# Causal softmax with 8-wide heads: mask and maximum from matrix products and reductions to fused vector operations

## What is computed

```python
q = _rope(q)
k = _rope(k)
att = jnp.einsum('bhqd,bhkd->bhqk', q, k) * (1.0 / np.sqrt(D))
causal = jnp.tril(jnp.ones((T, T), dtype=bool))
att = jnp.where(causal, att, -jnp.inf)
att = jax.nn.softmax(att, axis=-1)
y = jnp.einsum('bhqk,bhkd->bhqd', att, v)
```

## Time and profile before

| | |
|---|---|
| median of 3 runs | 2307.49 us (2306.52 to 2309.47) |
| the profiled execution | 2311.73 us, its span 2309.9 us |
| busy over the whole span | TensorE 2175.3 us (94%), VectorE 1691.0 (73%), ScalarE 1782.4 (77%), GpSimd 1432.2 (62%) |
| the stage of the change | about 213 to 546 us |

### The profile page before, as it was taken

One profiled execution on the slowest core, in us unless ns is written; L12 is line 12 of the kernel. 1 busy time (PEld: TensorE's weight loads), 2 busy tenths in 40 slices (PEclk: granted clock), 3 DMA queues, 4 the chain that ended last, 5 costly groups with the idle time before them and its releaser, 6 DMA issues. The chain is left out here.

```text
span 2309.9 us, 67166 instructions
## 1 busy us (share of the span) xinstructions
PE 2175.3 (94%) x22598; PEld 1606.6 (70%) x22598; DVE 1691.0 (73%) x3594; ACT 1782.4 (77%) x6112; POOL 1432.2 (62%) x1432
## 2 busy tenths in 40 slices
PE   6987999999698999999999999899999999999999
PEld 4984666665696788864788864675788864788863
DVE  5554888886554889973899974575899963899964
ACT  4774888986575999982899982556999982999982
POOL 4663777773663788860788860572788850888850
PEclk8997999999799999999999999999999999999999
DMA  6111000000113000000000000000000000000000
GB/s 248 43 40 42 2 0 0 0 1 24 40 43 120 9 9 7 9 0 5 9 9 7 9 1 0 2 0 6 9 9 7 9 0 5 9 9 7 9 1 37
DMA packets 22566, 45.93 MB, mean 20 GB/s; under 512 B 5344, under 2 KB 13792, under 8 KB 22048
## 3 DMA queue, kind: packets, MB, share of 16 engines
q1 hardware_dynamic: 17440, 34.01, 4.4%
q0 software_dynamic: 4992, 10.23, 1.5%
HBM read 24.44 MB, written 11.40 MB: 16 GB/s over the span
## 5 line engine op out<-in xcount | busy, mean ns | idle before, releaser
L279 POOL TENSOR_TENSOR space<-space 128x512 f32<-128x512 f32 x256 | 325.7, 1272 | 268.5 <-DVE space L382 268.1
L274 POOL TENSOR_TENSOR space<-space 128x512 f32<-128x512 f32 x256 | 267.6, 1045 | 126.1 <-ACT space L315 125.9
L329 ACT ACTIVATE space<-psum,space 128x128 f32<-128x128 f32 x1024 | 337.0, 385 | 1.7 <-DVE space L373 1.7
L1011 POOL TENSOR_TENSOR space<-space 128x256 f32<-128x256 f32 (+1 forms) x256 | 221.4, 886 | 85.2 <-DVE space L1113 83.1
L176 PE MATMUL psum<-big,space 128*128 128x256 f32 x1024 | 266.1, 382 | 6.8 <-issue 3.4
L268 POOL TENSOR_TENSOR space<-space 128x512 f32<-128x512 f32 x256 | 266.9, 1042 | 7.9 <-DVE space L353 7.3
L373 DVE TENSOR_REDUCE space<-psum 128x4 f32<-128x512 f32 x256 | 177.1, 692 | 98.0 <-PE psum L191 93.7
L1057 ACT ACTIVATE space<-psum,space 128x128 f32<-128x128 f32 (+1 forms) x512 | 210.3, 442 | 1.8 <-DVE space L1106 1.7
L329 ACT ACTIVATION_READ_ACCUMULATOR space<-psum,space 128x1 f32 x1024 | 201.8, 197 | 0.0
L176 PEld LDWEIGHTS psum<-big,space 128*128 128x128 f32 x1024 | 174.6, 190 | 28.4 <-issue 15.2
L676 ACT ACTIVATE big<-psum,wt 128x512 f32<-128x512 f32 (+1 forms) x96 | 65.4, 686 | 152.0 <-PE psum L653 151.9
(11 more groups left out here) (196 smaller groups left out, 5483.3 us busy)
## 6 DMA issues: line engine op xcount, KB each, us to landing
big<-early SPq DMA_DIRECT2D x1, 6944.0 KB, 27.5
rows<-space SPq DMA_DIRECT2D x16, 256.0 KB, 2.4
z<-token_y SPq DMA_DIRECT2D x16, 256.0 KB, 5.3
space<-z SPq DMA_DIRECT2D x64, 64.0 KB, 1.9
space<-z SPq DMA_DIRECT2D x64, 63.8 KB, 2.1
big<-late SPq DMA_DIRECT2D x1, 3114.0 KB, 13.7
x<-x_t SPq DMA_DIRECT2D x4, 512.0 KB, 5.2
x_final<-x SPq DMA_DIRECT2D x8, 256.0 KB, 2.1
```

What stands on the lines that cost most here:

```text
L274: pool.tensor_tensor(x, x, rn[:, (j - 1) % 2, :].unsqueeze(2).to_broadcast([P, 8, LD]), ALU.mult).then_inc(scaled, 1)
L279: pool.tensor_tensor(t3[:, j % 2, :], t1[:, j % 2, :], t2[:, j % 2, :], ALU.add).then_inc(summed, 1)
L329: ins = act.activation(pr[:, j % 2, h, t * P:(t + 1) * P], s_ps[h][:, t * P:(t + 1) * P], ACT.Exp, bias=nm[:, j % 2, h, t:t + 1], accum_ou ...
L1011: ins = pool.tensor_tensor(x, x, rl[:, ee % 2, t, :].unsqueeze(2).to_broadcast([P, 2, c1 - c0]), ALU.mult)
```

## The change

The mask leaves TensorE. The table `tri_q` becomes 384 columns wide (the triangle, zeros, the triangle) and holds -1e25 for masked places. In place of two reductions VectorE issues four fused operations `tensor_tensor_reduce`, one for each tile and head. Each adds the table (from SBUF) to the scores (from PSUM), multiplies by -1, writes the result to `pr` in SBUF, and gives the minimum of what it wrote, which is the negated maximum, to `nm`. ScalarE then takes the exponential in place in `pr`, with scale -1. The banks of scores are free once VectorE has read them (`nm_ready`), no more after the exponentials (`p_ready`). The wait for a free slot of `pr` (`pt_ready, s - 3`) moves from ScalarE to VectorE.

```diff
+FAR = 1e25
...
-    b["tri_q"] = (1 - seen.T) * MASKED
+    b["tri_q"] = np.concatenate([1 - seen.T, np.zeros((P, P)), 1 - seen.T], 1) * -FAR
...
                     if at_least(s, 2):
-                        pe.wait_ge(p_ready, s - 1)
-                    for n in range(2):
-                        mm(bank[n].rearrange("p (a n) -> p a n", a=4)[:, 0:4:2, :], g.ident[:, :], g.tri_q.unsqueeze(1).to_broadcast([P, 2, P]),
-                           start=True, stop=False, skip_group_check=True)
+                        pe.wait_ge(nm_ready, s - 1)
                     for t, cols in ((0, slice(0, P)), (1, slice(P, TRI))):
                         for n in range(2):
                             q = 2 * (e % 2) + n
                             r = slice(32 * q, 32 * q + 32)
-                            ins = mm(bank[n][:, cols], qz[r, k, jj, t * P:(t + 1) * P], qk[r, k, T:T + (t + 1) * P], start=False, stop=(t == 1), skip_group_check=True)
+                            ins = mm(bank[n][:, cols], qz[r, k, jj, t * P:(t + 1) * P], qk[r, k, T:T + (t + 1) * P], start=(t == 0), stop=(t == 1), skip_group_check=True)
...
                     act.wait_ge(nm_ready, u + 1)
-                    if at_least(u, 4):
-                        act.wait_ge(pt_ready, u - 3)
                     for t, (c0, c1) in enumerate(((0, P), (P, TRI))):
                         for h in range(2):
-                            ins = act.activation(pr[:, ee % SLOTS, h, c0:c1], s_ps[ee % 2][h][:, c0:c1], ACT.Exp,
-                                                 bias=nm[:, ee % 2, t, h:h + 1], accum_out=ls[:, ee % 2, t, h:h + 1])
+                            x = pr[:, ee % SLOTS, h, c0:c1]
+                            ins = act.activation(x, x, ACT.Exp, scale=-1.0, bias=nm[:, ee % 2, t, h:h + 1], accum_out=ls[:, ee % 2, t, h:h + 1])
...
+                    if not isinstance(s, int):
+                        for n in (-1, 1, 3):
+                            dve.compute_val(s - n)
+                    dve.wait_ge(v_zero, 1)
                     dve.wait_ge(s_ready, s + 1)
                     if at_least(s, 2):
                         dve.wait_ge(p_ready, s - 1)
-                    dve.tensor_reduce(nm[:, e % 2, 0, :], s_pair[e % 2][:, :, 0:P], AX.X, ALU.max, negate=True)
-                    dve.tensor_reduce(nm[:, e % 2, 1, :], s_pair[e % 2][:, :, P:TRI], AX.X, ALU.max, negate=True).then_inc(nm_ready, 1)
+                    if at_least(s, 4):
+                        dve.wait_ge(pt_ready, s - 3)
+                    for t, (c0, c1) in enumerate(((0, P), (P, TRI))):
+                        for h in range(2):
+                            ins = dve.tensor_tensor_reduce(pr[:, e % SLOTS, h, c0:c1], s_ps[e % 2][h][:, c0:c1], g.tri_q[:, c0:c1], -1.0, FAR,
+                                                           ALU.add, ALU.min, nm[:, e % 2, t, h:h + 1])
+                    ins.then_inc(nm_ready, 1)
```

More of the change, by code:

```diff
@@ L871, in small_head_softmax @@
     s_ps = ((g.bank[2], g.bank[3]), (g.bank[4], g.bank[5]))
-    s_pair = (g.bank_pair2, g.bank_pair4)
     pt_ps = (g.bank[6], g.bank[7])
@@ L1142, in free @@
     def free(eng, bank):
-        last = ((turned, B), (out_ready, B), (p_ready, U), (p_ready, U), (p_ready, U), (p_ready, U), (pt_low, U), (pt_high, U))
+        last = ((turned, B), (out_ready, B), (nm_ready, U), (nm_ready, U), (nm_ready, U), (nm_ready, U), (pt_low, U), (pt_high, U))
         eng.wait_ge(*last[bank])
```

## The result

The changed kernel takes 2298.06 us (median of 9 runs, 2294.92 to 2305.4) against 2307.97 us for the one before (9 runs on the same chip): ratio 0.9964, 95% interval 0.9953 to 0.9975. It is faster by 9.9 us. Forecast were 2311 us and no gain, with a chance of 0.33 for faster, so the sign is missed, although 2298 lies inside the range.

A forecast was written before the change was run, and what follows sets the result against it. TensorE was taken to bound the softmax stage, with VectorE taking its place after the change. Even part +8, last batch -2, first rounds -4 and end rounds +1 gave +3 us on the median 2307.5: 2311 us, range 2286 to 2359.

The forecast's parts named there:

- even part: 14 softmax batches from 242 to 522 us: VectorE's 20.4 + 0.2 us a batch against TensorE's 20.04, +8 us.
- last batch, and the ends: Last batch, without projection or rotation, still paced by TensorE: -2 us; last round's fused operations with nothing beside them: +0.53.
- first rounds, and the first fused operation: Seven low-clock rounds each lose mask products of 0.56 us, -4 us; first round's fused operations with nothing beside them, +0.53.
- The bound before: Softmax stage before the change: TensorE sets the pace, busy 20.00 of 20 us, a batch taking 20.04 us.
- What TensorE gives up: Two mask products a round leave TensorE, 2.5 us a batch, so it needs 17.5 and waits 2.5 to 3.
- The exchange on VectorE: Fused operations 1.10 us plus reads 0.36 replace reductions of 0.93: +0.53 us a round, VectorE 16.2 to 20.4 a batch.
- 0.2 us a batch for the waits between engines: Allowance in the even batches for VectorE waiting on ScalarE's exponentials, tight in the round with no extra operation.
- The price of SBUF: ScalarE's exponentials reading SBUF cost +0.024 us each, 0.8 us a batch, giving 18.6 of 20.4 us busy, hidden.
- Rival 1: VectorE's accumulator read is nearly free: 2292 us with 0.05 a read, 2283 with 0.03; chance 0.22.
- Rival 2: Each fused operation and read on VectorE holds the next for its full length: 2.10 us a round, 2384 us; chance 0.10.
- Rival 3: VectorE's fused operation has a fixed part 0.05 to 0.10 us larger than a reduction: 2335 to 2359 us; chance 0.17.
- Rival 4: TensorE stays longer at the low clock: ten such rounds more +16 us, a whole stage +200; chance 0.04.

The follow-up runs named there:

- before_total_first: Kernel before the change, with GpSimd's sum of the rotation (L997) moved ahead of its product in that round: 20.04 us a batch, 1.0001 of before.
- no_mask: Kernel before the change, with its two mask products on TensorE left out and nothing in their place: 18.68 us a batch, 0.9900 of before.
- exp_from_psum: Changed kernel with exponentials taken from the unmasked scores in PSUM, fused operations kept, banks held until the exponentials are done: 19.69 us a batch, 0.9977 of before.
- both_masks: Changed kernel with TensorE's two mask products kept ahead of the scores: 20.28 us a batch, 1.0013 of the kernel before.
- split_dve: Changed kernel with VectorE's copy of the transposed probabilities cut in three: 19.95 us a batch, 0.9982 of the kernel before.
- psum_in_place: Changed kernel with fused operations writing back into the PSUM bank of scores and exponentials reading PSUM again: 20.47 us a batch, 1.0022 of the kernel before.
- less_dve: Changed kernel with VectorE's copy of the transposed probabilities cut to 128 of 384 columns: 18.83 us a batch, 0.9908 of the kernel before.
- after_again: The changed kernel itself, run again on another chip as anchor: 19.69 us a batch, 0.9956 of the kernel before.
- split_act: Changed kernel with ScalarE's copy of the transposed probabilities cut in three of 128 columns: 19.69 us a batch, 0.9967 of the kernel before.
- less_act: Changed kernel with ScalarE's copy of the transposed probabilities cut to 128 of 384 columns: 19.69 us a batch, 0.9963 of the kernel before.

## Why the prediction was wrong

The forecast was +3 us, the stage measured -9.6. By the terms of its sum:

| term | forecast | measured |
|---|---|---|
| even part | +0.56 x 14 = +8 | 20.04 to 19.69: -0.35 x 14 = -4.9 |
| last batch, and the ends | -2 + 0.5 | -0.2 |
| first rounds, and the first fused operation | -4 + 0.5 | 34.99 to 30.47 for two batches: -4.5 |

**The bound before.** Right. before_total_first, which shortens the way that paces the changed kernel, gained nothing, and no_mask, which takes work from TensorE alone, gained 1.36 us a batch.

**What TensorE gives up.** Right: 17.5 us of work are left, and TensorE waits for VectorE's copy as forecast, if less (1.7 us a batch for 2.5 to 3). The 17.5 itself is a sum that no row measures: the record of TensorE in the changed kernel is busy 18.30 of 20 us, gaps' edges included.

**The exchange on VectorE: the step that failed.** "Four are 0.36 us." The fused operations' own part, 1.10 us, was measured at 1.11. The read was priced at 0.09 by ScalarE's read and VectorE's reciprocal; it costs 0.00, below even the bound of 0.03. So the exchange is +0.18 us a round, not +0.53, and the sum had 2.9 us a batch too much: VectorE needs 17.5 to 17.9 us, not 20.4, and stands idle 17.3 us between 260 and 500 us, 1.4 a batch, where the prediction called anything over 0.5 a sign that it was wrong. The mistake was one of kind. Neither neighbour was a VectorE accumulator read, and the bound from below was set at 0.03 with no row behind it, where nothing excluded zero. The even part's sign hung on this one price, and the text said so.

**The method of the sum: a second error, of the other sign.** With the read at zero the same method (fullest engine, plus 0.2) would give ScalarE's 18.6 + 0.2 = 18.8 us a batch and 2285 us, too fast by 13. The prediction gave 0.2 us a batch for the waits between engines; they are worth 1.1 over the fullest engine. While one engine was full, as TensorE was before (busy 20.00 of 20 us), its own work gave the batch. Once no engine is far ahead of the others, the loop through all of them does. no_mask shows the same in the kernel without any fused operation, 18.68 us against 17.5. The two errors partly cancelled: that the time fell inside the range is luck.

**ScalarE.** The price of SBUF was taken as 0.024 us from a pair of lengths (L568, L563), where the exponentials show 0.042 from start to start. That pair, without accumulator reads, gives 0.026 from start to start too (0.520 against 0.494), so it was the pair that misled, more than the lengths. The sum added its 0.8 us to 17.8 us of busy time, which from start to start were 17.2; these two errors cancel in the 18.6. That the price is hidden was right; exp_from_psum shows it.

**The rivals.** Rival 1 (the read is nearly free) is what happened, one step beyond its lower end; its time, 2283 to 2292, was too low since the loop took over. Rival 2, beside which the Trainium skill, "VectorE: DVE Perf Modes", section "The DRAIN you can't avoid", was named, is refuted: each operation starts 0.07 us before the record of the one ahead has ended. The prediction took that section at its first words; it goes on to say that an operation which is not held starts earlier. Rival 3 is refuted: the fixed part of a fused operation is that of a reduction. Rival 4, more rounds at the low clock, did not come about in the changed kernel. TensorE came back to the full clock earlier than before, in the changed kernel's stretches:

```profile
218.00:223.00 5.00, 5.00 (x24) 3.90 (x23) 4.12 (x21) 3.45 (x15) 4.28 (x7) 0.50 0.01 3
223.00:228.00 5.00, 5.00 (x38) 3.05 (x38) 2.68 (x12) 4.18 (x18) 3.76 (x4) 0.55 0.00 0
228.00:233.00 5.00, 4.68 (x51) 2.94 (x49) 4.17 (x22) 4.18 (x19) 2.67 (x5) 1.00 0.00 2
```

Counted in rounds it is the same: in both kernels the first six rounds run at the low clock (but for 214 to 218 us in the changed kernel, granted 0.90 while TensorE mostly waited), from 213.19 to 235.22 us before and from 209.13 to 227.62 us now, so a round is 0.59 us shorter where 0.56 was forecast. The first two batches took 30.5 and 30.9 us in the two profiles of the changed kernel, 29.3 to 31.7 in most variants, and 34.4 and 34.6 in the two others with mask products, both_masks and before_total_first. But split_dve and psum_in_place, without them, took 34.1 and 35.9: there TensorE stayed at half the clock for two or three rounds more. What decides this no run shows, so the -4.5 us are the forecast price only as long as that doesn't happen.

**Last batch.** VectorE's 2.0 us a round were forecast. It runs at 2.24 us (512.19 to 516.66 for two rounds of scores), for 2.32 before; here too TensorE waits for VectorE's copy (0.32 us in every second round). Of the 0.6 us that eight such rounds would save, the end of the stage gave back some 0.4, which no run takes apart. From the last projection to the end it is -0.5 us, of which the batch before the last has 0.35.

## What to carry to other kernels

When an edit takes work off the one full engine, the new time is not the next-fullest engine's work: walk back through the timeline from one repeated event to the one before, engine by engine, and count the waits between queues. Test whose work counts by adding and removing the same small amount on each engine in turn; an engine busy for 18.6 of 19.7 us may matter not at all, while one busy for 17.9 counts, here with a quarter (split_dve) to nearly half (less_dve) of the work added or removed. Where a sum's sign hangs on the price of one instruction that no row shows, its bound from below is zero until a row of that very instruction says otherwise.

## What was new about the hardware

- VectorE's read of an accumulator is 0.08 us long and takes nothing from start to start when the fused operation writes to SBUF: 0 in the median of 390 reads. With the result in PSUM the operation took 0.02 us (128 columns) to 0.04 us (256) longer, and the read still nothing. ScalarE's read costs 0.093 us.
- A fused add, scale, write and minimum over one PSUM and one SBUF source runs at the pace of a plain reduction: 0.21 us for 128 and 0.345 for 256 columns.
- A ScalarE exponential with bias and accumulator costs 0.042 us more from SBUF than from PSUM, whether over 128 or 256 columns. The pair of 512 columns without accumulator differs by 0.026.
- The mean length of a batch repeats across chips: 19.69 us, to 0.01, in five runs (the changed kernel, after_again, split_act, less_act and exp_from_psum), on whose chips the kernel before took 2287 to 2314 us. For an edit of one stage this distance tells far more than the median.
